# Loading W_in and the patterns as float32 and multiplying them as float32 on TensorE, instead of casting them to bfloat16 in the DMA

## What is computed

```python
normed_q = rms_norm(query_input, norm_query_w)
proj = normed_q @ W_in.T                      # W_in: 2048 x 2048 float32
q = proj.reshape(B, S, H, D) @ W_q.T          # W_q: 128 x 128, H = 16 heads, D = 128
k = stored_patterns @ W_k.T                   # patterns: 16 heads x 1024 x 128 float32
v = stored_patterns @ W_v.T
scores = jnp.einsum('bshd,hmd->bhsm', q * b, k)
probs = jax.nn.softmax(scores, axis=-1)
attn_out = jnp.einsum('bshm,hmd->bshd', probs, v)
```

## Time and profile before

| what | value |
|---|---|
| median of 2 runs | 2166.13 us (2164.64 to 2167.63) |
| the profiled execution's own time | 2167.92 us |
| span of its slowest core (core 6), first to last instruction | 2165.7 us |
| spans of the 8 cores | 2147.5 to 2165.7 us |
| mean granted TensorE clock of core 6 | 0.891 |
| TensorE matmul busy | 1804.8 us, 83% of the span |
| DVE / ACT / POOL busy | 240.3 / 607.3 / 146.6 us |

### The profile page before, as it was taken

The page is one execution under the profiler, slowest core; times in us unless marked ns, Lnnn a source line. Parts: engine busy times, 40 slices in busy tenths (PEclk is TensorE's granted clock), DMA queues, the critical chain, the costliest instruction groups (busy, mean ns, idle before and its releaser), DMA issues.

```text
span 2165.7 us, 20546 instructions; the slowest of 8 cores (2147.5 to 2165.7 us)
## 1 busy us (share of the span) xinstructions
PE 1804.8 (83%) x8488; PEld 839.3 (39%) x8488; DVE 240.3 (11%) x455; ACT 607.3 (28%) x596; POOL 146.6 (7%) x239
## 2 busy tenths in 40 slices
PE   2349958888841499999999999999997979899695
PEld 2224433443421244444444444444443434344242
DVE  3530000000038300000000000000000020100202
ACT  1351156556656211111111111111113212222120
POOL 1000010000002100000000000000000010000101
PEclk9559958888865699999999999999998989999898
DMA  7610050000024222222222222222213131221301
GB/s 164 151 20 1 0 78 1 1 1 1 1 97 165 88 78 78 78 78 78 78 78 78 73 70 72 78 78 78 78 59 102 39 102 39 78 64 39 99 23 58
DMA packets 42367, 142.06 MB, mean 66 GB/s; under 512 B 6181, under 2 KB 6182, under 8 KB 38950
## 3 DMA queue, kind: packets, MB, share of 16 engines
q0 software_dynamic: 28592, 96.58, 15.4%
q1 hardware_dynamic: 13686, 44.19, 6.3%
HBM read 103.10 MB, written 16.78 MB: 55 GB/s over the span
## 4 chain that ended last, share of the span: by engine, by line
PE 78%; ACT 7%; DVE 6%; DMA 5%; issue 3%; POOL 0%; DVEq 0%; ACTq 0%; POOLq 0%; SPq 0%
PE PS L936 21%; PE PS L951 20%; PE PS L1076 19%; PE PS L462 5%; PE PS L547 3%; PE PS L562 2%; DMA out<-arena 2%; ACT arena L591 2%; PE PS L611 1%; DMA arena<-patT 1%; DVE arena L323 1%; PE PS L584 1%; PE PS L578 1%; ACT arena L439 1%; ACT arena L386 1%
## 5 line engine op out<-in xcount | busy, mean ns | idle before, releaser
L1076 PE MATMUL PS<-arena 128*128 128x512 bf16 x1956 | 451.9, 386 | 55.0 <-DVE arena L1015 44.3
L936 PE MATMUL PS<-arena 128*128 128x512 bf16 x2048 | 455.1, 381 | 5.6 <-DMA arena<-wu 5.6
L951 PE MATMUL PS<-arena 128*128 128x512 bf16 x1984 | 438.7, 379 | 0.0
L1076 PEld LDWEIGHTS PS<-arena 128*128 128x128 bf16 x1956 | 193.5, 99 | 298.1 <-issue 75.2
L936 PEld LDWEIGHTS PS<-arena 128*128 128x128 bf16 x2048 | 200.8, 98 | 249.2 <-issue 9.1
L951 PEld LDWEIGHTS PS<-arena 128*128 128x128 bf16 x1984 | 194.3, 98 | 234.0
L960 ACT ACTIVATE arena<-PS,sgc_s 128x1024 bf16<-128x1024 f32 x64 | 71.3, 1114 | 735.5 <-PE PS L945 735.5
L1043 ACT ACTIVATE arena<-arena 128x2048 bf16<-128x2048 int8 x64 | 121.8, 1908 | 351.7 <-PE PS L1065 342.0
L591 ACT ACTIVATE arena<-PS 128x1024 bf16<-128x1024 f32 x128 | 129.3, 1024 | 60.6 <-PE PS L578 60.6
L968 DVE TENSOR_TENSOR arena<-arena 128x1024 bf16<-128x1024 bf16 x64 | 44.3, 693 | 851.4 <-ACT arena L963 851.4
L462 PE MATMUL PS<-arena 128*128 128x512 bf16 x496 | 117.6, 391 | 8.2 <-ACT arena L439 8.2
(11 more groups left out here) (110 smaller groups left out, 927.4 us busy)
## 6 DMA issues: line engine op xcount, KB each, us to landing
arena<-wg POOLq DMA_DIRECT2D x64, 512.0 KB, 3.5
arena<-wu POOLq DMA_DIRECT2D x64, 512.0 KB, 4.2
arena<-x SPq DMA_DIRECT2D x16, 1024.0 KB, 5.2
arena<-wd SPq DMA_DIRECT2D x64, 256.0 KB, 2.6
arena<-win POOLq DMA_DIRECT2D x16, 512.0 KB, 6.8
x1sp<-arena SPq DMA_DIRECT2D x8, 1024.0 KB, 4.2
arena<-x1sp POOLq DMA_DIRECT2D x32, 256.0 KB, 5.1
out<-arena POOLq DMA_DIRECT2D x32, 256.0 KB, 3.5
```

What stands on the lines that cost most here:

```text
L936: En.matmul(PG[:, half * 512:half * 512 + 512], wgb[:, hc * 128:(hc + 1) * 128], x1nT3[:, hc, half * 512:half * 512 + 512], start=(hc == 0 ...
L951: En.matmul(PU2[:, half * 512:half * 512 + 512], wub[:, hc * 128:(hc + 1) * 128], x1nT3[:, hc, half * 512:half * 512 + 512], start=(hc == ...
L1076: En.matmul(PS[:, j * 512:(j + 1) * 512], fuse3[:, ic, j * 128:(j + 1) * 128], wdb[:, c * 512:(c + 1) * 512], start=(ic == 0), stop=(ic == ...
```

## The change

W_in and the pattern tiles are loaded as float32 by the SP queue, without a cast, into the larger buffers O_WINF and O_PATF that the arena map already had. The three small matrices are loaded a second time, as float32 (wqT32, wkT32, wvT32), and the matmuls of the fold (L313, L307) and of stage 3 (L500, L495, L512, L508) take float32 operands on both sides. Shapes, counts and the order on TensorE, ScalarE and VectorE stay as they are; the loads' semaphores change from sB and sCm to sW.

```diff
+        dma(Ry, dC, wqT32[:], wqT_d)
+        dma(Ry, dC, wkT32[:], wkT_d)
+        dma(Ry, dC, wvT32[:], wvT_d)
...
         for i in range(2):
-            dma(Rg, sB[i], ARbf[:, (163840 + i * 4096) // 2:(163840 + i * 4096) // 2 + 2048],
+            dma(Ry, sW[i], ARf[:, (172032 + i * 8192) // 4:(172032 + i * 8192) // 4 + 2048],
                 win_d[i])
...
         def win_load(h):
-            winb = bfv(O_WIN[h % 2], 2048)
+            winf = f32v(O_WINF[h % 2], 2048)
             if h >= 2:
-                wait(Rg, cT, fold_mm_val[h - 2])
-            dma(Rg, sB[h % 2], winb, win_d[h])
-            win_ld[h] = sB[h % 2].n
+                wait(Ry, cT, fold_mm_val[h - 2])
+            dma(Ry, sW[h % 2], winf, win_d[h])
+            win_ld[h] = sW[h % 2].n
...
                            En.matmul(PF[:, ec * 128:(ec + 1) * 128],
-                                     winb[:, ec * 128:(ec + 1) * 128],
-                                     wqT[:], start=True, stop=True))
+                                     winf[:, ec * 128:(ec + 1) * 128],
+                                     wqT32[:], start=True, stop=True))
...
-        wait(Rg, bar, bar.n)
+        wait(Ry, bar, bar.n)
...
-            pat = bfv(O_PAT[h % 2], 1024)
+            pat = f32v(O_PATF[h % 2], 1024)
...
             if h >= 2:
-                wait(Rg, cT, e_mm_val[h - 2])
-            dma(Rg, sCm[h % 2], pat, patT_d[h])
+                wait(Ry, cT, e_mm_val[h - 2])
+            dma(Ry, sW[h % 2], pat, patT_d[h])
...
-                       En.matmul(PK[:, half * 512:half * 512 + 512], wkT[:],
+                       En.matmul(PK[:, half * 512:half * 512 + 512], wkT32[:],
                                  pat[:, half * 512:half * 512 + 512], start=True, stop=True))
...
                        En.matmul(PV[:, mc * 128:(mc + 1) * 128], pat[:, mc * 128:(mc + 1) * 128],
-                                 wvT[:], start=True, stop=True))
+                                 wvT32[:], start=True, stop=True))
```

More of the change, by code:

```diff
@@ L80, in _build_nc @@
         wvT = ctx.enter_context(nc.sbuf_tensor("wvT_s", [128, 128], BF16))
+        wqT32 = ctx.enter_context(nc.sbuf_tensor("wqT32_s", [128, 128], F32))
+        wkT32 = ctx.enter_context(nc.sbuf_tensor("wkT32_s", [128, 128], F32))
+        wvT32 = ctx.enter_context(nc.sbuf_tensor("wvT32_s", [128, 128], F32))
         nqw = ctx.enter_context(nc.sbuf_tensor("nqw_s", [128, EC], F32))
@@ L263, in _build_nc @@
         for i in range(2):
-            dma(Rg, sB[i], ARbf[:, (163840 + i * 4096) // 2:(163840 + i * 4096) // 2 + 2048],
+            dma(Ry, sW[i], ARf[:, (172032 + i * 8192) // 4:(172032 + i * 8192) // 4 + 2048],
                 win_d[i])
-            pre_win_ld.append(sB[i].n)
+            pre_win_ld.append(sW[i].n)
             dma(Ry, sA[i], ARf[:, (131072 + i * 8192) // 4:(131072 + i * 8192) // 4 + 2048],
@@ L287, in win_load @@
         def win_load(h):
-            winb = bfv(O_WIN[h % 2], 2048)
+            winf = f32v(O_WINF[h % 2], 2048)
             if h >= 2:
-                wait(Rg, cT, fold_mm_val[h - 2])
-            dma(Rg, sB[h % 2], winb, win_d[h])
-            win_ld[h] = sB[h % 2].n
+                wait(Ry, cT, fold_mm_val[h - 2])
+            dma(Ry, sW[h % 2], winf, win_d[h])
+            win_ld[h] = sW[h % 2].n
         def emit_fold(h):
-            winb = bfv(O_WIN[h % 2], 2048)
-            wait(Rt, sB[h % 2], win_ld[h])
+            winf = f32v(O_WINF[h % 2], 2048)
+            wait(Rt, sW[h % 2], win_ld[h])
             src3 = PF.rearrange("p (ec d) -> p ec d", d=128)
@@ L305, in emit_fold @@
                     if ec8 == 7:
-                        Rt(lambda En, winb=winb, ec=ec:
+                        Rt(lambda En, winf=winf, ec=ec:
                            En.matmul(PF[:, ec * 128:(ec + 1) * 128],
-                                     winb[:, ec * 128:(ec + 1) * 128],
-                                     wqT[:], start=True, stop=True).then_inc(cT.h, 1))
+                                     winf[:, ec * 128:(ec + 1) * 128],
+                                     wqT32[:], start=True, stop=True).then_inc(cT.h, 1))
                     else:
                         cT.n -= 1
-                        Rt(lambda En, winb=winb, ec=ec:
+                        Rt(lambda En, winf=winf, ec=ec:
                            En.matmul(PF[:, ec * 128:(ec + 1) * 128],
-                                     winb[:, ec * 128:(ec + 1) * 128],
-                                     wqT[:], start=True, stop=True))
+                                     winf[:, ec * 128:(ec + 1) * 128],
+                                     wqT32[:], start=True, stop=True))
                 if hf == 1:
@@ L484, in _build_nc @@
             if h >= 2:
-                wait(Rg, cT, e_mm_val[h - 2])
-            dma(Rg, sCm[h % 2], pat, patT_d[h])
-            ldv = sCm[h % 2].n
-            wait(Rt, sCm[h % 2], ldv)
+                wait(Ry, cT, e_mm_val[h - 2])
+            dma(Ry, sW[h % 2], pat, patT_d[h])
+            ldv = sW[h % 2].n
+            wait(Rt, sW[h % 2], ldv)
             if h >= 2:
@@ L508, in _build_nc @@
                        En.matmul(PV[:, mc * 128:(mc + 1) * 128], pat[:, mc * 128:(mc + 1) * 128],
-                                 wvT[:], start=True, stop=True).then_inc(cT.h, 1))
+                                 wvT32[:], start=True, stop=True).then_inc(cT.h, 1))
                 else:
```

## The result

The changed kernel takes 2214.11 us (median) against 2167.45 us before, measured together: a ratio of 1.0215, with a 95% interval of 1.0200 to 1.0231. That is +46.6 us, or slower by 2.1%. Some executions of either kernel, in which the cores of one die had a lower clock, took several per cent longer; all ratios, and the medians in the table of the experiments, are taken without them, and by those medians the difference is 44.7 us.

What follows compares the result with a forecast made beforehand. Stages 1 and 3 were taken as bound by chains of waits and load round trips, not TensorE throughput. Terms 29.6 + 1.5 + 9 - 1.5 = +38.6 us on the 2166.1 us median gave 2205 us, range 2190 to 2222.

Steps and rivals of the forecast that it cites:

- the line of 2%: Whole kernel: smallest slowdown a measurement can tell from no change, 43 us, at 2209.5 us; 0.55 for slower than that.
- the two dear rivals: Stages 1 and 3: clock stays low for float32 (2296 us, 0.17), or load and stream don't overlap (2291 us, 0.10).
- What a float32 matmul costs: Folds and stage 3: two passes, each streaming at twice bfloat16 time; 128 columns 0.427 us at 1.2 GHz, 512 columns 1.71.
- one column a cycle: 512-column matmuls in stage 3 cost half the forecast, folds the same; 2197 us, chance 0.09.
- no overlap: Folds and stage 3: weight load and stream run one after the other; +125 us, 2291 us, chance 0.10.
- one pass: Both stages: float32 matmuls run in one pass of reduced precision; +3 us, 2169 us, chance 0.03.
- The clock: TensorE in stages 1 and 3: clock rises from 0.50 to 1.00 about 4.4 us after a dense run starts.
- the first of the two dear rivals: Stages 1 and 3: the clock stays low for float32 work; +130 us, 2296 us, chance 0.17.
- Stage 1: Folds: slower float32 matmuls add 4.2 us an iteration, +29.6 us over seven; the first iteration adds 1.5, between 0 and 5.
- Loads in stage 1: W_in and x loads on the SP queue stay hidden; if not, waits on win of up to 5 us an iteration.
- Stage 3: Pattern loads run beside the other head's matmuls, 3.6 us a head; +9 us, +7.5 to +21 by load landing time.
- Stage 4: Its first matmuls, entered at clock 1.00 instead of 0.50, save about 1.5 us.

Runs made afterwards that it cites:

- the four-times kernel: Changed kernel's float32 loads, matmuls reading upper halves as bfloat16, each fold matmul issued four times, against the kernel before: 2189.89 us, ratio 1.0134.
- The filler: Changed kernel plus 140 unread matmuls ahead of each tile's transposes in stage 1: 2189.90 us, ratio 1.0129 to before, where the changed kernel had 1.0228.
- loads alone: Changed kernel's float32 loads, queues and buffers, but matmuls read only upper halves as bfloat16, against the kernel before: 2160.94 us, ratio 0.9994.
- The four-buffer run: Changed kernel with four pattern buffers instead of two, beside the changed kernel on the third chip: 2229.26 us against 2228.43.

## Why the prediction was right, and where it was off

The forecast was 2205 us with its own range of 2190 to 2222 and the line of 2% in it; the measured 2214.1 lies in that range, and on the side of the line to which 0.55 was given, though the interval of the ratio touches it. That side was partly luck: 0.27 of the 0.55 belonged to the two dear rivals, which are out, and the forecast itself lay on the other side. The sum came to +38.6 where +46.6 was measured, and most of what it lacked is stage 3.

*What a float32 matmul costs.* Right. The two passes are seen as two records, a pass of 128 columns takes 0.213 us at the low clock and 0.111 at the high one, and the guess that no row supported, twice the bfloat16 time to stream a pass, was right: 1.71 and 0.86 us for 512 columns, as forecast. The rule of the Trainium skill in "FP8 and Floating Point Precision", section TensorE Precision Notes, four passes for a true float32 product, agrees with that and with the four-times kernel; the halved output rate of "Perfetto Trace Analysis", section Engine Utilization, taken as the whole price, does not. With that the rivals of one column a cycle, of no overlap and of one pass are out.

*The clock.* Right in kind: float32 passes raise it like others, so the first of the two dear rivals is out as well: stage 3 begins with float32 matmuls alone and stands at 1.00 from 311.5, 5 us later. In the iteration shown it rose 5.1 us after the transposes, where I took 4.4, and an iteration is 19.2 us, where I had 19.0 from an iteration of 14.8 that took 15.0 in the mean. The filler shows what the low clock costs in stage 1, 14.7 us, of which at most 9 belong to the change. What I did not see coming is a clock of 0.81 on two of the chips.

*Stage 1.* +29.6 forecast for seven iterations, +29.2 measured. The first one cost +3.4 and not +1.5, within the 0 to 5 that I gave: the second W_in load, which stands behind x on one queue, took 13.8 us to land, so that the second fold began at 20.8 us, 0.9 later than before, in spite of a first fold that began 1.4 us earlier. So the first fold's slower matmuls did not cover that load, as I had said; the rest is the second fold's slower matmuls, since with loads alone the first transpose came only 1.1 us later.

*Loads in stage 1.* Right from the second iteration on: hidden, shown by the kernel with loads alone. The one wait after the first fold is that of the second, 1.3 us in the changed kernel.

*Stage 3.* Here is the term that was mis-sized: "From there a load with its signals (3.6 us) runs beside the other head's 3.5 us: 3.6 us a head", and with it "What hides the loads now is TensorE's own time". +9 was forecast. The like of it, from the first load's issue to stage 4, went from 56.0 us to 72.0 on the core shown (301.94 to 373.93): +16. With two buffers the load of a head begins only when that buffer's own matmuls are done, so two heads take a load, its signals and one head's matmuls. That is the mechanism of the forecast, and its sizes were short: the loads in this core's chain took 3.45 to 4.10 us where I had 3.4; its signals took 0.3 where I had 0.2, and the first matmul after a wait 1.10 instead of 0.86. So fourteen heads took 55.8 us, 4.0 a head, not 50.4: 5.4 us of the 7 that were missing. Another 1.2 is the first load, 4.6 us to the first matmul instead of 3.4. TensorE's own time did not hide the loads: load and signals were longer than the other head's 3.5 us, and each tenth of a microsecond more went into the time of two heads. The four-buffer run shows that the load's share of the changed stage is 6 to 8 us.

*Stage 4.* -1.5 forecast, -2.0 seen, but its cores scatter by 10 us in one run, so this was not tested.

The terms of the forecast as measured: 29.2 + 3.4 + 15.9 - 2.0 = +46.5. That this meets the +46.6 of the ratio is chance: with the two rows that the forecast left at nothing, -0.2 and -2.1, it is +44.2.

## What to carry to other kernels

A float32 matmul of 128 or 512 columns cost four bfloat16 ones on TensorE here, at either clock; loading float32 and reading its upper half with a step of two did without that price (0.9994), with truncated operands. Spare time on an engine that is not the bottleneck is not free to spend when it sits inside a chain that alternates between engines: stage 1 had TensorE two thirds idle and still lost 29 us. And where two buffers alternate, compare the load's round trip with the work on the other buffer before anything else: doubling the pattern buffers gave the kernel before 17 us, more than a third of what the change cost.

## What the runs showed of the hardware that I had not expected

The granted clock has a third level in the rows, 0.81. On the second and third chip it was granted in stage 1 and after of every kernel with float32 folds, on all cores in stage 1 and on some pairs of cores for much longer: the changed kernel's folds of 0.111 us a pass then took (139.28 - 137.14) / 16 = 0.134:

```profile
137.14 2.04 PE L319 MATMUL PS<-wqT_s,arena 128*128 128x128 f32 x14
...
139.28 2.04 PE L319 MATMUL PS<-wqT_s,arena 128*128 128x128 f32 x14
```

That makes the same kernel 2228 us in one measurement and 2211 to 2212 in two others, with before at 2161 to 2167 in all four: the change costs 2.2% or 3.0%. In these runs the level goes with the chip; that the chip decides is not shown. The Trainium skill, "TensorE: Matmul & The Clock Gate", Part 1, describes a peak-current limit at 13/16 of the clock (0.81) for a die with three cores in dense matmuls. The level agrees. That it must come does not: on the first chip core 6 ran 105 us of dense matmuls in stage 2 at 1.00, and stage 2 was as short on the other seven cores. What draws it stays open. It is not float32 alone, since two cores of the kernel before with four buffers had it too on the third chip, after some 50 to 60 us and through half of stage 2, here core 0:

```profile
163.00:209.00 46.00, 46.00 (x177) 19.09 (x176) 0.00 (x0) 6.39 (x6) 0.00 (x0) 0.81 0.00 0
```

The run that was to decide, four bfloat16 matmuls for one float32, fell on a chip where no profiled execution showed it.
